# Routing weights of a two-of-six mixture: second best taken from the exponentials, two chains side by side, 19 vector operations for 23

## The reference, cut to what matters

```python
rh = relu(features @ router_w1 + router_b1)
expert_logits = softmax(rh @ router_w2 + router_b2)      # six per token
top_w, top_i = top_k(expert_logits, 2)
routing_weights = softmax(top_w)                          # two per token
h1 = relu(features @ expert_w1 + b1); h2 = relu(h1 @ expert_w2 + b2)
expert_out = h2 @ expert_w3 + b3                          # all six
combined = sum(take(expert_out, top_i) * routing_weights)
```

## Time and profile before

| what | value |
|---|---|
| median of 3 runs | 664.72 us (664.31 to 666.39) |
| profiled execution | 664.7 us |
| its span, first to last instruction | 662.7 us |
| PE busy | 638.3 us, 96% |
| DVE busy | 542.7 us, 82% |
| ACT busy | 476.7 us, 72% |
| POOL busy | 278.1 us, 42% |
| share of the last chain on PE, DVE, ACT | 77%, 10%, 6% |
| mean granted clock of PE | 0.995 |

### The profile page before, as it was taken

How to read it: one execution, slowest core, us unless ns; L and a number is a source line. 1 busy time by engine, 2 the same in 40 slices (tenths; PEclk the granted TensorE clock), 3 DMA queues, 4 the chain that set the end, 5 groups by cost and what they waited for, 6 DMA issues and landing times.

```text
span 662.7 us, 27520 instructions
## 1 busy us (share of the span) xinstructions
PE 638.3 (96%) x11956; PEld 366.0 (55%) x11956; DVE 542.7 (82%) x1096; ACT 476.7 (72%) x1216; POOL 278.1 (42%) x359
## 2 busy tenths in 40 slices
PE   8799999999999999999999999999999999999885
PEld 7355665545655556555565456555565555555563
DVE  6698777898798987988788987989879887867777
ACT  3788875876778775987758767787759875788442
POOL 4353115316653095323853166530953237311182
PEclk9999999999999999999999999999999999999997
DMA  5000000000000001000100001000010001000001
GB/s 177 1 2 2 2 2 4 3 2 2 19 2 3 2 3 18 2 3 3 19 2 2 2 3 19 2 2 2 3 19 2 2 4 18 2 2 2 4 3 34
DMA packets 9720, 6.75 MB, mean 10 GB/s; under 512 B 8704, under 2 KB 9088, under 8 KB 9472
## 3 DMA queue, kind: packets, MB, share of 16 engines
q1 hardware_dynamic: 9600, 5.00, 3.0%
HBM read 2.90 MB, written 2.10 MB: 8 GB/s over the span
## 4 chain that ended last, share of the span: by engine, by line
PE 77%; DVE 10%; ACT 6%; issue 4%; DMA 1%; POOL 0%; SPq 0%; ACTq 0%; DVEq 0%; POOLq 0%
PE s_bank L621 31%; PE s_bank L587 28%; ACT p L919 5%; PE s_bank L719 3%; PE s_bank L601 3%; PE s_bank L837 3%; DVE nmax L1092 2%; PE s_bank L800 2%; PE s_bank L811 2%; DVE e2t L1349 1%; PE s_bank L731 1%; ACT g L925 1%; DMA e2t<-ids 1%; PE s_bank L650 1%; DVE gt L1280 1%
## 5 line engine op out<-in xcount | busy, mean ns | idle before, releaser
L919 ACT ACTIVATE p<-s_bank,nmax 128x512 f32<-128x512 f32 x512 | 346.9, 690 | 123.0 <-DVE nmax L1092 118.5
L1092 DVE TENSOR_REDUCE nmax<-s_bank 128x1 f32<-128x512 f32 x512 | 325.4, 683 | 41.4 <-PE s_bank L587 39.7
L587 PE MATMUL s_bank<-kf,g 64*64 64x512 f32 x2048 | 255.7, 591 | 1.6 <-DVE g L1207 0.8
L621 PE MATMUL s_bank<-p,woz 64*64 64x256 f32 x4096 | 244.8, 376 | 1.2 <-ACT p L919 1.2
L621 PEld LDWEIGHTS s_bank<-p,woz 64*64 64x64 f32 x4096 | 156.2, 133 | 113.4 <-issue 37.3
L416 POOL TENSOR_TENSOR woz<-cst,rz 128x256 f32<-128x256 f32 x126 | 74.6, 613 | 231.3 <-DVE rz L1098 231.3
L587 PEld LDWEIGHTS s_bank<-kf,g 64*64 64x64 f32 x2048 | 74.9, 133 | 84.7 <-issue 38.6
L919 ACT ACTIVATION_READ_ACCUMULATOR p<-s_bank,nmax 128x1 f32 x512 | 105.8, 207 | 0.0
L1449 POOL TENSOR_TENSOR st<-st,power 128x8 f32<-128x8 f32 (+3 forms) x25 | 38.6, 1545 | 87.5 <-DVE st L1119 87.5
L1104 DVE STREAM_TRANSPOSE m<-s_bank 128x512 f32<-128x512 f32 x64 | 45.9, 717 | 31.1 <-PE s_bank L621 30.7
L425 POOL TENSOR_TENSOR y<-y,gt 128x768 f32<-128x768 f32 x28 | 41.2, 1472 | 0.5 <-DVE y L1364 0.5
(11 more groups left out here) (143 smaller groups left out, 522.1 us busy)
## 6 DMA issues: line engine op xcount, KB each, us to landing
tower_out<-o SPq DMA_DIRECT2D x16, 128.0 KB, 2.6
cst<-consts SPq DMA_DIRECT2D x1, 1070.0 KB, 8.2
e2t<-ids SPq DMA_DIRECT2D x1, 768.0 KB, 5.4
cst<-consts SPq DMA_DIRECT2D x1, 352.0 KB, 6.0
cst<-consts SPq DMA_DIRECT2D x1, 256.0 KB, 3.6
e2t<-ids SPq DMA_DIRECT2D x1, 192.0 KB, 2.8
cst<-consts SPq DMA_DIRECT2D x1, 128.0 KB, 2.3
e2t<-ids SPq DMA_DIRECT2D x1, 64.0 KB, 2.0
```

Source lines behind the costliest of these rows:

```text
L587: last = pe.matmul(double[half(q), 512 * r:512 * r + 512], g[half(r), a // 2 % 2, a % 2, first:first + 64], kf[half(r), par, a // 4, :], s ...
L621: last = pe.matmul(bank("PV", i, a)[half(q), 512 * hh:512 * hh + 256], woz[half(r), kept, 2 * mm + hh, :], keys[:, q, :, :], start=(part = ...
L919: nc.scalar.activation(p[:, 8 * kept + c % 8, :], bank("S", i, c - r)[:, 512 * r:512 * r + 512], ACT.Exp, bias=nmax[:, c % 16:c % 16 + 1], ...
L1092: nc.vector.tensor_reduce(nmax[:, c % 16:c % 16 + 1], bank("S", i, c - r)[:, 512 * r:512 * r + 512], AX.X, ALU.max, negate=True).then_inc( ...
```

## The change: what it does

The order of DVE's operations and two waits change; all slot tables stay.

- The first of the best (`G(3)`, `V(4)`, `G(4)`) is found from the logits less their maximum, where the best is exactly zero, and no longer from the normalised probabilities. Part 1 therefore no longer waits for ACT's exponential.
- The second best is the maximum of the exponentials with the best reduced by 2, and the weights' difference is (second - 1) / sum. The normalised probabilities are no longer made.
- Part 2 waits for the exponential and has four operations; part 3 has four, of which two (one of 48, one of 8 elements) don't wait for one another; part 4 has one; part 5 has four; part 6 has one. Before, the parts had 2, 3, 3, 3, 5, 4, 3 operations; now 2, 3, 4, 4, 1, 4, 1.
- ACT's second exponential waits for count 11, in part 3, and no longer for count 16, in part 4.

```diff
-        GATE = 22
+        GATE = 18
...
-                    act.wait_ge(u.gate, GATE * u.n + 16)
+                    act.wait_ge(u.gate, GATE * u.n + 11)
...
+                stt = nc.vector.scalar_tensor_tensor
                 if part == 1:
+                    after(2)
+                    done(3, stt(out=G(3), in0=G(0), scalar=0.0, in1=rank, op0=ALU.is_equal, op1=ALU.mult))
+                    after(3)
+                    done(4, red(V(4), G(3), AX.X, ALU.max))
+                    after(4)
+                    done(5, tt(G(4), G(3), bcast(V(4)), ALU.is_equal))
+                if part == 2:
                     dve.wait_ge(u.gate_act, 2 * u.n + 1)
-                    done(3, red(V(1), G(1), AX.X, ALU.add))
-                    after(3)
-                    done(4, nc.vector.reciprocal(V(2), V(1)))
-                    after(4)
-                    done(5, tt(G(2), G(1), bcast(V(2)), ALU.mult))
-                if part == 2:
+                    done(6, red(V(1), G(1), AX.X, ALU.add))
                     after(5)
-                    done(6, red(V(3), G(2), AX.X, ALU.max))
+                    done(7, stt(out=G(5), in0=G(4), scalar=-2.0, in1=G(1), op0=ALU.mult, op1=ALU.add))
                     after(6)
-                    done(7, tt(G(3), G(2), bcast(V(3)), ALU.is_equal))
+                    done(8, nc.vector.reciprocal(V(2), V(1)))
                     after(7)
-                    done(8, tt(G(3), G(3), rank, ALU.mult))
+                    done(9, red(V(5), G(5), AX.X, ALU.max))
                 if part == 3:
...
                     after(9)
-                    ...
+                    done(10, tt(G(6), G(5), bcast(V(5)), ALU.is_equal))
+                    done(11, stt(out=V(6), in0=V(5), scalar=-1.0, in1=V(2), op0=ALU.add, op1=ALU.mult))
                     after(10)
+                    done(12, tt(G(6), G(6), rank, ALU.mult))
+                    after(12)
+                    done(13, red(V(8), G(6), AX.X, ALU.max))
                 if part == 4:
...
                     after(13)
+                    done(14, tt(G(7), G(6), bcast(V(8)), ALU.is_equal))
+                if part == 5:
+                    dve.wait_ge(u.gate_act, 2 * u.n + 2)
+                    done(15, nc.vector.tensor_scalar(V(9), V(7), 1.0, None, ALU.add))
                     after(14)
+                    done(16, tt(G(2), G(7), bcast(V(7)), ALU.mult))
                     after(15)
+                    done(17, nc.vector.reciprocal(V(3), V(9)))
+                    after(16)
+                    done(18, tt(G(2), G(2), G(4), ALU.add))
                 if part == 6:
+                    after(18)
                     wait(dve, y_pool, units[min(u.u, PAIRS - 1)].pool0)
+                    tt(G(8), G(2), bcast(V(3)), ALU.mult).then_inc(u.gated, 1)
```

More of the change, by code:

```diff
@@ L1281, in gating @@
                     after(7)
-                    done(8, tt(G(3), G(3), rank, ALU.mult))
+                    done(9, red(V(5), G(5), AX.X, ALU.max))
                 if part == 3:
-                    after(8)
-                    done(9, red(V(4), G(3), AX.X, ALU.max))
                     after(9)
-                    done(10, tt(G(4), G(3), bcast(V(4)), ALU.is_equal))
+                    done(10, tt(G(6), G(5), bcast(V(5)), ALU.is_equal))
+                    done(11, stt(out=V(6), in0=V(5), scalar=-1.0, in1=V(2), op0=ALU.add, op1=ALU.mult))
@@ L1288, in gating @@
                     after(10)
-                    done(11, nc.vector.scalar_tensor_tensor(out=G(5), in0=G(4), scalar=-2.0, in1=G(2), op0=ALU.mult,
-                                                            op1=ALU.add))
+                    done(12, tt(G(6), G(6), rank, ALU.mult))
+                    after(12)
+                    done(13, red(V(8), G(6), AX.X, ALU.max))
                 if part == 4:
-                    after(11)
-                    done(12, red(V(5), G(5), AX.X, ALU.max))
@@ L1294, in gating @@
-                    after(12)
-                    done(13, tt(G(6), G(5), bcast(V(5)), ALU.is_equal))
                     after(13)
-                    done(14, tt(G(6), G(6), rank, ALU.mult))
+                    done(14, tt(G(7), G(6), bcast(V(8)), ALU.is_equal))
+                if part == 5:
+                    dve.wait_ge(u.gate_act, 2 * u.n + 2)
+                    done(15, nc.vector.tensor_scalar(V(9), V(7), 1.0, None, ALU.add))
                     after(14)
-                    done(15, red(V(8), G(6), AX.X, ALU.max))
@@ L1300, in gating @@
-                    done(16, tt(V(6), V(5), V(3), ALU.subtract))
-                if part == 5:
+                    done(16, tt(G(2), G(7), bcast(V(7)), ALU.mult))
                     after(15)
-                    done(17, tt(G(7), G(6), bcast(V(8)), ALU.is_equal))
-                    dve.wait_ge(u.gate_act, 2 * u.n + 2)
-                    done(18, nc.vector.tensor_scalar(V(9), V(7), 1.0, None, ALU.add))
+                    done(17, nc.vector.reciprocal(V(3), V(9)))
+                    after(16)
@@ L1306, in gating @@
+                    done(18, tt(G(2), G(2), G(4), ALU.add))
+                if part == 6:
                     after(18)
[L1307 to L1314, removed]
@@ L1315, in gating @@
                     wait(dve, y_pool, units[min(u.u, PAIRS - 1)].pool0)
-                    tt(G(8), G(0), G(1), ALU.add).then_inc(u.gated, 1)
+                    tt(G(8), G(2), bcast(V(3)), ALU.mult).then_inc(u.gated, 1)
             def ffn(u, slot):
```

## The result

The changed kernel takes 661.81 us (median of 4 runs, 661.28 to 662.33), the kernel before in the same session 664.94 (4 runs, 664.31 to 666.39). The ratio is 0.9943, 95% interval 0.9931 to 0.9956. The profiled execution took 661.28 us, its span is 659.4 where it was 662.7, its mean granted clock 0.998 where it was 0.995. The interval leaves no doubt that the change helps; its size is half a per cent.

The account below looks back on a forecast made before the run. PE was taken to bound the pairs, mutual waits among engines the tail, from L1266's end on. 664.7 - 1.4 (L1266) - 0.15 (ACT) - 1.85 (clock) - 0.2 (pairs) = 661.1 us, range 660.0 to 664.6.

Parts of the forecast that it names:

- L1266 of 7b, -1.4 us: In the tail, DVE's changed gating lets L1266 of 7b end 1.4 us earlier; ends 0.5 and 1.75.
- The toss-up at part 1: 7a's first part 1 operation against POOL's L433: L1364 starts about 640.85 if it wins, 641.46 if it loses; 641.15 taken.
- The second rival: In the tail, small operation and those behind it lose to POOL, L1266 no earlier: -0.2 us, 664.5; chance 0.10.
- ACT, -0.15: In the tail, ACT's eight relus start 0.16 us after L1266's end and not 0.32: 0.15 us more.
- The clock, -1.85: In the tail, PE's 1.70 us pause shrinks to about 0.3, PE keeps 2.4 GHz: 1.85 us; ends 0 and 2.0.
- The six pairs, -0.2: Pairs with table F: slot 40's maximum 0.17 us earlier to 0.1 later, six times that -1.0 to +0.6; -0.2 taken.
- The third rival: Slot 39 of six pairs: scalar_tensor_tensor loses to POOL's woz, L1349 up to 0.6 us later: +3.6, 666.75; chance 0.07.
- The first rival: PE's clock falls in the tail all the same, so the time is 663.0 us; chance 0.28.
- What was called hidden: Tail behind L1266: gating ends 4.0 us after it, first L1376 5.0, the second waits for PE at 5.2: costs nothing.
- The rule that the prediction drew from the earlier trace: DVE with two SBUF inputs beside POOL: whoever starts first goes ahead, the other waits; leads of 0.01 to 0.05 us decide.
- The last stretch: Tail from the second L1376 to the end, 8.9 us; a change would mean the tail was read wrongly.

Follow-up runs that it names:

- e8: The changed kernel with two reductions that nobody reads ahead of the comparison of part 3, in 7a alone; 661.71 us (one run).
- e3: The kernel before with twelve unread 128x128 products in PE's pause before the last L811 of 7a; 664.33 us (12 runs), ratio 0.9995.
- e6: The kernel before with six unread products in PE's pause before the last L811 of 7a; 663.88 us (12 runs), ratio 0.9982.
- e2: The kernel before with the new gating for pairs 0 to 6 only, the old one for 7a and 7b; 663.61 us (12 runs), ratio 0.9987.
- e5: The changed kernel run once more, unaltered, against the kernel before; 662.14 us (9 runs), ratio 0.9954.
- e9: The changed kernel with POOL's last five sums of pair 6 held back until L1266 of 7b; 662.27 us (8 runs), ratio 0.9966.
- e10: The changed kernel with part 0 of 7b ahead of part 4 of 7a in DVE's order; 661.52 us (4 runs), ratio 0.9944.

## Why the prediction was right

The span fell by 3.3 us, where the sum had 3.6. That it came so close is in part luck: the pairs gave 0.8 us more than forecast and L1266 0.2 more, the clock 0.4 less, and 0.8 us were lost in two stretches for which the prediction had no term (+0.27 and +0.55 in the table). The main terms, though, were the right ones, in the right order.

**L1266 of 7b, -1.4 us: right, by the steps given.** Seen -1.43 and, with parts 1 and 2, -1.59. The toss-up at part 1 fell on the good side (L1272 639.15, L433 639.16, 0.18 us); the prediction gave no reason why it should, so this is luck, by a lead of 0.01 us that e8 (639.39 and 639.40) repeats. L1288 and L1289 led, L1291 paid for L425, L1296 for L433. T came 3.91 behind L1357, forecast 3.98. The second rival (collisions eat the tail, 664.5) falls with it; e8 shows that even a comparison that starts later doesn't bring it about.

**ACT, -0.15: right.** The relus start 0.16 us after T (644.99 and 644.83).

**The clock, -1.85: right mechanism, 0.4 us too large.** T to the second weights product fell by 1.62, ACT's 0.15 in it, where I had 2.0. The distance is 5.58, not 5.2: I gave the first eight bias products 0.65 us, and from their start (646.67, 1.84 behind T) to that of the output product it is 0.87 by the chain of waits; the sixteen took 1.4 for 1.3. (The terms as I wrote them add up to 5.12, not 5.2.) That PE's standing still was the cause is shown by e3 and e6, not by the change alone. At the same clock, 0.998 or more, the changed kernel took 661.3 us (4 runs, two sessions) and the kernel before 663.6 (11 runs): of the 3.1 us by medians some 0.8 (3.1 less 2.3, an estimate) are the clock's, and the rest is an earlier T, the relus and the pairs. The profile before, at 0.995, showed the fall whole, and my sum compared with that. The median shows less of it, since the clock varies from run to run: 0.997 or more in 11 of 64 before and in 8 of 13 after, 0.995 or less in 42 of 64 and in 3 of 13.

**The six pairs, -0.2: the direction right, the size wrong.** They gave -0.97 (e2: -0.86). The maximum of slot 40 comes 5.59 us after part 0's start and not 5.79, so 0.20 earlier, just beyond the early end of my -0.17 to +0.1. Each contact went the good way or cost what was forecast: L1272 0.69 us (forecast 0.7), L1281 ahead of woz, L1289 paying 0.60. The mistake was to book the middle of two ends when the row had L1281 0.05 us ahead, on the early side. The third rival (slower by slot 39) needed +0.26 us a pair and got -0.20: PEld's wait is 0.7, not over 1.2. What I gave away here pays for what the clock's term lacked, and for +0.55 us between L811 of pair 6 and L1132, for which I had no term.

**That +0.55** is not shown to be the change's, nor the opposite. The same stretch takes 18.77 to 19.19 us in the four profiles with the old gating throughout, 19.03 to 19.90 in the nine with the new one somewhere, 19.74 after, 19.33 in e5 (the changed kernel again) and 19.90 in e2. A pause of 0.24 to 0.81 us stands in it inside one run of the output products, where PE waited for nothing that the profile shows; it is 0.53 before and 0.81 after, half of the difference. The cause stays open, and so does that of the +0.27 ahead of the first L1262, which comes at 129.78 to 131.10 us in the profiles without a fall before it, whichever gating they have.

**The first rival (the clock falls all the same, 663.0)** holds for some executions. Of 13 runs of the changed kernel 8 had 0.997 or more, 2 had 0.996 and 3 had 0.995. The one fall of this kernel of which a profile exists lies in pair 0, far from the tail (the windows of e5 above); where it lay in the others is open. The Trainium skill (TensorE: Matmul & The Clock Gate, "Part 1: The HAM clock gate") says that the monitor runs freely and does not start anew with a kernel; that one program has a fall in one execution and none in another, behind the same pause (e5), agrees.

**What was called hidden** was: DVE waits 0.84 us for ACT's second exponential of 7b, the first L1369 is done 4.9 us after T, and the second still waits 0.67 for PE. The last stretch takes 9.0 us (8.9).

**Who starts first.** The rule that the prediction drew from the earlier trace rows held in the changed kernel and misled in e8: a start of 0.03 us behind POOL's recorded one still won. The Trainium skill (SBUF — State Buffer, "Who interferes with whom") has the exclusion of the two; e9 agrees (0.20 for 1.47 us without POOL). "Starts first", read from recorded starts, can't be told for leads of some hundredths of a us: 0.03 behind won in e8, 0.01 (L1289) and 0.06 (L1291) behind lost.

## What to carry to other kernels

Beside an engine that holds a shared port, count the operations left behind the end of its last long instruction and not those that were dropped: here POOL's L425 and L433 absorbed most of what was dropped, and the gain came from the five operations between L433 and L1262 that now stand ahead of its end or are gone. Look what a wait of another engine does to PE, and price its pause twice, once as time and once as the clock that may follow, which differs from run to run; a few unread products in the pause show which it is. And take off a wait with an eye on the next in line: once L1266 was early, an even earlier one (e9, e10) did not bring the relus forward (4.05 to 4.07 us after the weights product in all three).

## What the hardware showed that was not expected

An operation on 6 to 8 elements per partition with two SBUF inputs can wait out nearly the whole of POOL's instruction beside it (0.60 us for 8 elements beside one of 0.61, 1.44 us for 6 beside one of 1.55). A DVE operation and POOL's can both go ahead when they start close together: in e8 one that began 0.03 us behind POOL's kept its 0.19 us and POOL stretched by 0.08. And among runs of the kernel before the time goes with the mean clock: 663.6 us at 0.998 or more (11 runs), 664.6 at 0.996 (11), 665.1 at 0.994 to 0.995 (32), 667.1 at 0.991 to 0.993 (10), means of each group. From the first group to the last 0.006 of 663 us is 4.0 us, and the time differs by 3.5. So a good part of the scatter of single runs, from 662.8 to 668.1 us, goes with PE's clock.
